# A gated attention and mixture-of-experts block: two expert steps between the last attention stages, the gating and maximum products in another order, and the residual added last

## What is computed

```python
x = x + tanh(g_xattn) * attention(layernorm(x), ctx, ctx)   # 32 query heads of 16, 8 key/value heads
z = layernorm(x)
logits = tanh(z @ Wg1.T) @ Wg2.T                            # 8 experts
scores = softmax over the two largest logits, 0 elsewhere
h = silu(z @ Wup[e].T + bup[e]);  y_e = h @ Wdown[e].T + bdown[e]
x = x + tanh(g_ffn) * sum over e of scores[e] * y_e
```

## Time and profile before

| what | before |
|---|---|
| timed runs, median | 796.16 us |
| the profiled execution | 791.42 us |
| its span, first to last instruction | 789.6 us |
| mean granted TensorE clock | 0.946 |
| TensorE busy | 675.6 us |
| VectorE busy | 551.0 us |
| ScalarE busy | 380.1 us |
| GpSimd busy | 293.7 us |

### The profile page before, as it was taken

One profiled execution on the slowest core, in us unless ns is written; L12 is line 12 of the kernel. 1 busy time (PEld: TensorE's weight loads), 2 busy tenths in 40 slices (PEclk: granted clock), 3 DMA queues, 4 the chain that ended last, 5 costly groups with the idle time before them and its releaser, 6 DMA issues.

```text
span 789.6 us, 17887 instructions
## 1 busy us (share of the span) xinstructions
PE 675.6 (86%) x5232; PEld 463.6 (59%) x5232; DVE 551.0 (70%) x1541; ACT 380.1 (48%) x706; POOL 293.7 (37%) x406
## 2 busy tenths in 40 slices
PE   3789999999999999998889699999999998979600
PEld 2445545455455554554443488889998997768500
DVE  3567878778787787878873466777766766766635
ACT  2366766666676666766653133333333334433300
POOL 4123445454454545545432400000000026665564
PEclk9999999999999999999996689999999999898955
DMA  4622434344443443434221754444456468999898
GB/s 152 211 84 88 140 129 137 125 141 137 129 138 123 141 137 127 137 126 139 71 104 54 271 189 155 151 144 156 145 167 201 148 228 270 312 326 305 280 350 277
DMA packets 67847, 135.15 MB, mean 171 GB/s; under 512 B 8640, under 2 KB 12736, under 8 KB 67520
## 3 DMA queue, kind: packets, MB, share of 16 engines
q1 hardware_dynamic: 46432, 81.28, 30.8%
q0 software_dynamic: 10240, 33.56, 12.4%
q10 hardware_dynamic: 11104, 19.42, 8.0%
HBM read 76.04 MB, written 58.20 MB: 170 GB/s over the span
## 4 chain that ended last, share of the span: by engine, by line
PE 69%; DVE 14%; DMA 8%; POOL 3%; issue 3%; ACT 1%; DVEq 0%; SPq 0%; POOLq 0%
PE s_ps L987 12%; DVE nmax L770 10%; PE bank_a L966 8%; PE st_ps L1010 7%; DMA r_in<-x_scratch 5%; PE st_ps L1120 4%; PE st_ps L1121 4%; PE st_ps L1122 4%; PE bank_c L1027 4%; PE s_ps L1104 4%; DMA out<-r_in 3%; PE bank_b L975 3%; PE st_ps L1018 2%; POOL y_late L514 2%; PE bank_b L1133 2%
## 5 line engine op out<-in xcount | busy, mean ns | idle before, releaser
L770 DVE TENSOR_REDUCE nmax<-s_ps 128x8 f32<-128x1024 f32 x128 | 156.2, 1220 | 83.7 <-PE s_ps L987 83.3
L545 ACT ACTIVATE probs<-st_ps 128x1024 f32<-128x1024 f32 x128 | 131.2, 1025 | 109.7 <-PE st_ps L1018 106.1
L987 PE MATMUL s_ps<-k_t,q_t 32*128 32x256 f32 x1024 | 151.6, 414 | 35.4 <-DVE nmax L770 32.7
L1010 PE MATMUL st_ps<-q_t,k_t 32*128 32x512 f32 x512 | 147.9, 652 | 0.8 <-ACT probs L545 0.7
L987 PEld LDWEIGHTS s_ps<-k_t,q_t 32*128 32x128 f32 x1024 | 92.1, 191 | 86.0 <-DVE nmax L770 47.3
L493 POOL DMA_INDIRECT y<-expert_out,rows_all x42 | 41.3, 983 | 193.1 <-DMA expert_out<-y_sb 183.4
L1120 PE MATMUL st_ps<-w_hi,zh 128*128 x312 | 96.0, 308 | 0.6 <-DVE zl L891 0.6
L1121 PE MATMUL st_ps<-w_lo,zh 128*128 x312 | 88.9, 285 | 0.0
L1122 PE MATMUL st_ps<-w_hi,zl 128*128 x312 | 88.6, 284 | 0.0
L629 ACT ACTIVATE t_sb<-u_sb 128x256 f32<-128x256 f32 x78 | 32.6, 418 | 104.5 <-DVE u_sb L899 104.5
L470 POOL DMA_INDIRECT slots<-z,slot_i x64 | 64.2, 1004 | 16.4 <-issue 16.1
(11 more groups left out here) (149 smaller groups left out, 1420.3 us busy)
## 6 DMA issues: line engine op xcount, KB each, us to landing
expert_out<-y_sb SPq DMA_DIRECT2D x78, 256.0 KB, 2.8
z_s<-slots ACTq DMA_DIRECT2D x74, 256.0 KB, 2.7
x_in<-in_x SPq DMA_DIRECT2D x32, 256.0 KB, 2.7
wst<-in_w SPq DMA_DIRECT2D x32, 256.0 KB, 2.6
x_res<-in_x SPq DMA_DIRECT2D x32, 256.0 KB, 2.9
x_scratch<-x_res SPq DMA_DIRECT2D x32, 256.0 KB, 2.0
r_in<-x_scratch SPq DMA_DIRECT2D x21, 256.0 KB, 4.6
out<-r_in SPq DMA_DIRECT2D x21, 256.0 KB, 4.5
```

The costliest lines, as they stand in the source:

```text
L545: a.activation(out, st_ps[:, :].rearrange("t (k n) -> t k n", k=2), ACT.Exp, scale=HD ** -0.5).then_inc(exp_done[half], 1)
L770: v.tensor_reduce(out, s_ps[:, :].rearrange("s (r g c t) -> s r g c t", r=2, g=2, c=2), X_AXIS, ALU.max, negate=True).then_inc(max_done, 1)
L987: last = t_.matmul(s_ps[:, HALF * rr + 2 * P * gg:HALF * rr + 2 * P * (gg + 1)], q_t[r2][row:row + ROWS32, P * g_:P * (g_ + 1)], k_t[r2][r ...
L1010: t_.matmul(st_ps[:, HALF * rr:HALF * (rr + 1)], k_t[r][row:row + ROWS32, P * i:P * (i + 1)], q_t[r][row:row + ROWS32, :], start=True, sto ...
```

## The change

It has three parts.

1. In the attention steps the gating layer stands elsewhere: the first gating product behind `scores(1)` and the ranking, the second behind `scores(2)`; ScalarE's tanh behind the copy of the attention output; VectorE's copy of the logits behind z and MAX8 behind the reciprocal. In each score block the maximum product comes first on its array rows, then the transposed scores, and the last pair of `s_ps` is issued last.
2. Expert steps 1 and 2 are run between attention steps 36 and 37 and between 37 and 38, before the barrier; the second part starts with step 3. For this `zh`, `zl`, `u_sb`, `t_sb`, `hh`, `hl` and `y_sb` get memory over attention buffers that are free by then, with waits for those.
3. In mixing y2 is gathered first and scaled as before; VectorE computes y1 = y1 * coefficient + y2 one step later, without the residual; GpSimd adds the residual. Stores and residual loads stand one step later, and the mixing runs from step 58 to 80.

```diff
 def mixed_at(s):
-    return [... MIX0 + m * (TILES + 3 - MIX0) // (NA - 1) == s]
+    return [... MIX0 + m * (TILES + 2 - MIX0) // (NA - 1) == s]
...
 # SyncE
-                for m in mixed_at(s - 2 if isinstance(s, int) else s):
+                for m in mixed_at(s - 3):
                     store_mixed(m)
-                for m in mixed_at(s - 3 if isinstance(s, int) else s):
+                for m in mixed_at(s - 4):
...
 # GpSimd
-                for j, (y, done, read) in enumerate(((y1, y1_loaded, mix1), (y2, y2_loaded, mix2))):
+                for j, (y, done, read) in enumerate(((y2, y2_loaded, mix1), (y1, y1_loaded, mix2))):
...
+                    pool.wait_ge(r_loaded[n % RRING], 16 * (n // RRING + 1))
                     pool.wait_ge(mix1, n + 1)
-                    pool.wait_ge(scaled, n + 1)
-                    g.tensor_tensor(r_in[n % RRING][:, :], r_in[n % RRING][:, :], y2[n % YRING][:, :],
+                    g.tensor_tensor(r_in[n % RRING][:, :], r_in[n % RRING][:, :], y1[n % YRING][:, :],
...
 # VectorE
-                for m in mixed_at(s):
...
-                    dve.wait_ge(r_loaded[m % RRING], 16 * (m // RRING + 1))
+                for m in mixed_at(s - 1):
+                    dve.wait_ge(scaled, m + 1)
                     dve.wait_ge(y1_loaded[m % YRING], 16 * (m // YRING + 1))
-                    v.scalar_tensor_tensor(r_in[m % RRING][:, :], y1[m % YRING][:, :], coef[0][:, m:m + 1],
-                                           r_in[m % RRING][:, :], ALU.mult, ALU.add).then_inc(mix1, 1)
+                    v.scalar_tensor_tensor(y1[m % YRING][:, :], y1[m % YRING][:, :], coef[0][:, m:m + 1],
+                                           y2[m % YRING][:, :], ALU.mult, ALU.add).then_inc(mix1, 1)
...
 # TensorE (the other engines alike)
-            pipeline(pe, step, STEPS, LOOP0, NA + O_SLOT, RING)
-            pe.drain().then_inc(phase1_over, 1)
-            pe.wait_ge(phase1_over, 4)
...
+            pipeline(pe, step, STEPS - 2, LOOP0, NA + O_SLOT, RING)
+            pe.wait_ge(tab_done[0], 2)
+            pe.wait_ge(max_done, 4 * B)
+            tile_step(1, 1, False)
+            step(STEPS - 2, (STEPS - 2) % RING)
+            pe.wait_ge(exp_done[0], 2 * B)
+            pe.wait_ge(exp_done[1], 2 * B)
+            pe.wait_ge(w_lo_done, B)
+            tile_step(2, 2, False)
+            step(STEPS - 1, (STEPS - 1) % RING)
+            pe.drain().then_inc(phase1_over, 1)
+            pe.wait_ge(phase1_over, 4)
+            tile_pipeline(pe, tile_step, 3)
```

More of the change, by code:

```diff
@@ L74, in pipeline, with tile_pipeline @@
         step(s, s % unroll)
-def tile_pipeline(eng, step):
-    for s in range(TILES + 4):
+def tile_pipeline(eng, step, first=0):
+    for s in range(first, TILES + 4):
         step(s, s % 16, s == 0)
@@ L93, in mixed_at @@
 def mixed_at(s):
-    return [m for m in range(NA) if isinstance(s, int) and MIX0 + m * (TILES + 3 - MIX0) // (NA - 1) == s]
+    return [m for m in range(NA) if isinstance(s, int) and MIX0 + m * (TILES + 2 - MIX0) // (NA - 1) == s]
 def block_kernel(nc, x_d, ctx_d, gx_d, gf_d, wg1_d, wg2_d, w_d, bup_d, bdn_d, out_d):
@@ L164, in block_kernel @@
         nmax = [sb(f"nmax{i}", [P, H], F32, p1) for i in range(2)]
-        nm_parts = sb("nm_parts", [P, D], BF16, p1)
-        nm_t = [sb(f"nm_t{i}", [P, D], BF16, p1) for i in range(2)]
         tooth = sb("tooth", [P, PAIRS], F32, p1)
@@ L202, in block_kernel @@
         bdn = sb("bdn", [P, E * D], F32, p23)
+        zh = [sb(f"zh{i}", [P, D], F32R, p23) for i in range(2)]
+        zl = [sb(f"zl{i}", [P, D], F32R, p23) for i in range(2)]
+        u_sb = [sb(f"u_sb{i}", [P, HE], F32, p23) for i in range(2)]
+        t_sb = [sb(f"t_sb{i}", [P, HE], F32, p23) for i in range(2)]
+        hh = [sb(f"hh{i}", [P, HE], F32R, p23) for i in range(2)]
+        hl = [sb(f"hl{i}", [P, HE], F32R, p23) for i in range(2)]
+        y_sb = [sb(f"y_sb{i}", [P, D], F32, p23) for i in range(2)]
         r_in = [sb(f"r_in{i}", [P, D], F32, p23) for i in range(RRING)]
@@ L387, in _ @@
             for s in (TILES + 4, TILES + 5):
-                for m in mixed_at(s - 2):
+                for m in mixed_at(s - 3):
                     store_mixed(m)
@@ L595, in step @@
                     a.activation(w_hi[:, bass.ds(s * WCHUNK, WCHUNK)], wst[:, :], ACT.Copy).then_inc(w_hi_done, 1)
-            pipeline(act, step, STEPS, LOOP0, NA + O_SLOT, RING)
-            act.wait_ge(gap_done, B)
-            act.drain().then_inc(phase1_over, 1)
-            act.wait_ge(phase1_over, 4)
-            act.wait_ge(tab_done[0], 2)
-            for b in range(NA - RING, NA):
-                act.wait_ge(scattered[b % RING], ring4(b, b % RING, 32))
-            a.activation(egap[:, :], gap_all[:, :], ACT.Exp).then_inc(exp2_done, 1)
             def tile_step(s, u, fresh):
@@ L635, in tile_step @@
                                  scale=coef[1][:, m:m + 1]).then_inc(scaled, 1)
-            tile_pipeline(act, tile_step)
+            pipeline(act, step, STEPS - 2, LOOP0, NA + O_SLOT, RING)
+            act.wait_ge(pv_done, 2 * B)
+            act.wait_ge(on_done, 2 * B)
+            act.wait_ge(st_done[1], 2 * B)
+            act.wait_ge(nmt_done, B)
+            act.wait_ge(tab_done[0], 2)
+            for b in range(NA - RING, NA):
+                act.wait_ge(scattered[b % RING], ring4(b, b % RING, 32))
+            tile_step(1, 1, False)
+            step(STEPS - 2, (STEPS - 2) % RING)
+            tile_step(2, 2, False)
+            step(STEPS - 1, (STEPS - 1) % RING)
+            act.wait_ge(gap_done, B)
+            act.drain().then_inc(phase1_over, 1)
+            act.wait_ge(phase1_over, 4)
+            a.activation(egap[:, :], gap_all[:, :], ACT.Exp).then_inc(exp2_done, 1)
+            tile_pipeline(act, tile_step, 3)
         @block.vector
@@ L1046, in step @@
                 if valid(b6):
+                    pe.wait_ge(zt_copied, b6 + 1)
+                    for c in range(DC):
+                        last = t_.matmul(bank_c[0:E, 0:S], wg1[:, c * E:(c + 1) * E], z_t[:, P * c:P * c + P],
+                                         start=(c == 0), stop=(c == DC - 1))
+                    last.then_inc(lg1_done, 1)
+                scores(2)
+                if valid(b6):
                     pe.wait_ge(th_done, b6 + 1)
                     t_.matmul(bank_c[:, 0:E], th_sb[:, :], wg2[:, :], start=True, stop=True).then_inc(lg2_done, 1)
-                scores(2)
                 if valid(b4):
```

85 lines of the change are left out of this document (39 added, 46 removed).

## The result

The changed kernel takes 818.7 us (median of 4 runs, 818.1 to 819.3), the kernel before 796.15: a ratio of 1.028 (95% interval 1.023 to 1.033). Some executions of every kernel have a lower mean clock and take longer, and the ratios leave them out. The changed kernel is slower by 2.8%; I forecast 785, and the time lies outside my range. Its profiled execution took 818.1 us, span 816.3, where the one before had 789.6.

What follows compares the result with a forecast made beforehand. TensorE was taken to bound attention, with attention stages, seam and mixing to price: -6.8 + 0 + 1.5 - 6 = -11.3 us, from 791.4 to 780 profiled, 785 us as timed median; range 774 to 806.

Steps and rivals of the forecast that it cites:

- Maximum products moved, 0: Attention score blocks: reordering products inside one group of array rows costs nothing; good-side bound -6 us.
- the equal 0.97 us: Score blocks: transposed scores to maximum product take 0.97 us with or without score pairs, read as groups not slowing one another.
- score pairs in order: Rival, attention: each block's last score pair ends 0.23 us later, giving +9.7 us in all, 806 us; chance 0.15.
- My bound of 0.23 a block: Score blocks, bad side: the last score pair waits its turn and ends 0.23 us later.
- clock: Rival, mixing: spread waits keep TensorE at 1.2 GHz longer, 14 more us at half clock cost 7: 792; chance 0.1.
- Gating layer moved, -0.27 a stage: Attention: -0.55 + 0.25 + 0.03 us a stage over 25 stages, -6.8 us; bounds -13.8 and 0.
- the context transpose's 0.03: Attention stage: the context transpose waits 0.03 us more for VectorE's logits copy, ready at 3.24 against TensorE's 3.21.
- The cover of the first gating product: Attention, between score blocks 1 and 2: ranking and first gating product end at 313.15, just before block 2 at 313.25.
- Seam, +1.5: Attention to experts: running the first two expert steps early costs more than it hides, +1.5 us; bounds -2.8 and +3.1.
- Mixing, -6: Mixing: adding the residual last on GpSimd saves half of a possible 0 to 12 us.
- mixing gives nothing: Rival, mixing: ScalarE waits for the y2 gather instead of VectorE's residual wait, DMA share stays 0.89: 791; chance 0.2.
- the 0.93 that I looked for: Sign of being right, mixing: DMA share of 0.93 or more from 650 us to the end of the tiles.

Runs made afterwards that it cites:

- e1: Kernel before with only the maximum products moved (first in their group, last score pair issued last): 796.4 us, ratio 1.001.
- e10: Kernel before with gating layer, mixing and early expert steps changed, and two small GpSimd products between its scatters; maximum products as before: 785.5 us, ratio 0.986.
- e8: Changed kernel with two 128x1 products added on GpSimd between its two scatters: 799.7 us, ratio 1.003.
- e14: Kernel before with gating layer and mixing changed, two GpSimd products between scatters, and VectorE's logits copy right behind the third maximum: 775.1 us, ratio 0.972.
- e6: Changed kernel with the maximum products alone put back as before: 789.7 us, ratio 0.992.
- e13: Changed kernel with four 128x1 products ahead of GpSimd's first scatter: 814.4 us, ratio 1.019.
- e17: Kernel before, unchanged, profiled again: 794.8 us.
- e7: Kernel before with gating layer and mixing changed, the other two edits left out: 787.0 us, ratio 0.990.
- e2: Kernel before with the gating layer alone moved: 793.6 us, ratio 0.998.
- e3: Kernel before with expert steps 1 and 2 alone put between the last attention stages: 798.4 us, ratio 1.002.
- e9: Kernel before with gating layer and mixing changed, and two 128x1 GpSimd products between its scatters: 784.3 us, ratio 0.985.
- e4: Kernel before with the mixing alone changed: 791.5 us, ratio 0.994.
- e5: Kernel before with gating layer and maximum products both moved, early expert steps and mixing as before: 816.3 us, ratio 1.022.
- e18: Changed kernel with two GpSimd products between the scatters (as e8), profiled again: 797.7 us.

## Why the prediction was wrong

Distances between the starts of the score blocks, medians of six batches (12, 15, 16, 19, 20, 23; all six are late in the changed kernel), show where each step of mine went:

| us from block to block | 1 to 2 | 2 to 3 | 3 to 4 | 4 to 1 | stage |
|---|---|---|---|---|---|
| before | 3.63 | 2.50 | 3.66 | 2.50 | 12.29 |
| e1 (products) | 3.53 | 2.65 | 3.61 | 2.65 | 12.44 |
| e10 (gating layer, scatters apart) | 3.00 | 2.50 | 4.16 | 2.50 | 12.16 |
| e8 (both, scatters apart) | 3.00 | 2.65 | 4.31 | 2.65 | 12.61 |
| after | 2.99 | 2.65 | 4.31 | 3.34 | 13.31 |
| e14 (copy early) | 3.00 | 2.50 | 3.75 | 2.50 | 11.75 |

- **Maximum products moved, 0: this step failed, and it decides.** I took the equal 0.97 us between two products of one group, with and without score pairs beside them, for independence of the groups. It only says that they stream side by side. The last score pair waits its turn behind the transposed scores: the maximum starts 1.37 us behind its block, not 1.22, and the exponential, which now waits for those transposed scores, comes just ahead of it at 1.31. The rule that I cited against me ("TensorE: Matmul & The Clock Gate", Part 3, The mechanism, of the Trainium skill) has matmuls end in program order, and these starts agree with it. Putting the products alone back in the changed kernel (e6) takes 29 us off by the ratios. In e8 it costs 0.45 us a stage against e10, in three blocks, as my rival "score pairs in order" had it, at 0.15 each and not 0.23. Alone (e1) it costs a third, since the transposed scores end earlier and two other distances shrink. My bound of 0.23 a block was wide enough for this; I gave it 0.15 of the chances. By the ratios e10, the change without this step and with the scatters apart, has -11.5 us, e8 +2.4 and the changed kernel +22: so the order costs 14 us by itself and 20 more by what follows.
- **What neither forecast nor rival had** is the last column: 2.65 to 3.34, the late signal. The later signal (1.37) and GpSimd's second scatter (with the gating layer moved it starts 1.33 us behind the block, before 1.55) met within 0.1 us. With the scatters apart the profiled execution has 9.2 us less by the last query transpose, which the 15 delays of 0.55 to 0.73 us account for, and 12.0 less in the drain, which runs at half clock from 433.8 us on in the one and nearly all at full in the other. The first part is shown to be the late signals' doing. The second isn't: e13 has the slow drain without them, so its cause stays open. The rival "clock" looked for a loss in the mixing and there was none (0.99 from 680 to 780 us; the kernel before had 0.93 from 650 to 750 in the earlier trace rows and 0.98 in e17); it came in the drain.
- **Gating layer moved, -0.27 a stage.** The first distance gained 0.63 (I had 0.55), the third lost 0.50 where I had 0.28: of the thin margins, the context transpose's 0.03 was 0.26 in e7 and 0.49 in the row of 280.64. Net it is -0.13. (The stages of the kernel before that I took as 12.24 each are 12.25 to 12.45, 12.32 in the mean; that changes little.) In e2 the late exponential and the slightly late maximum hide it (its stage is 12.33 in these batches): 1.7 us in all, which isn't told from nought. Moving the copy gives more than the rest: -0.54 a stage in e14. The cover of the first gating product held, as the row of 275.79 shows.
- **Seam, +1.5.** 1.2 between the last z transpose and the first expert result. The gating product of batch 31 starts at 473.17, 4.1 us behind the last z transpose, where it was 1.15 (440.7 to 441.85): 2.9 late where I had 3.6. Alone it is +3.1 with an interval that holds nought (e3), and beside the other edits +1.2 (e10 against e9), which isn't told from nought either.
- **Mixing, -6.** -3.9 in e4 (interval 0.3 to 0.8% of the time). VectorE's 19.7 us of waiting are gone. GpSimd waits 13.2 us for the residual, and ScalarE, which waited 0.6 us for its gather, now waits 15.9 ahead of its scaling, as the rival "mixing gives nothing" had it, but for less than VectorE had. The DMA share from 680 to 780 us is 0.90, under the 0.93 that I looked for. ScalarE's scaling in the changed kernel:

```profile
L628 ACT ACTIVATE y<-y,coef 128x512 f32<-128x512 f32 x21 | 15.1, 718 | 15.9 <-DMA y<-expert_out,rows_all 11.8 <-issue 4.1
```

Three of the four steps together came near the whole sum that I forecast (e10: -11.5 us, mine -11.3), in part by luck, since their single sizes differ from mine and e10 has the scatters apart as well. The rest of the loss is one step put at nothing and an interaction, and a sum of single steps has no place for an interaction.

## What to carry to other kernels

Put the matmul whose signal the next engine waits for ahead of others in program order, even if they use other rows of the array. Two edits that are each worth nothing can cost 20 us together (e1, e2 and e5); part of it here is that they move two engines against each other by a few tenths. So look at what else is issued within 0.1 us of a signal on the critical path, and measure edits in pairs as well as alone. Where two indirect DMAs follow each other at once beside such a path, try a gap between them. And take more than one profile of a kernel before pricing its stages: two of the kernel before differ by 0.25 us a stage.

## What was not expected of the hardware

- Semaphore signals of TensorE often come late when they fall due 1.0 to 1.5 us behind the start of a GpSimd scatter: by 0.1 to 0.3 us if due up to 1.31 behind it, and by 0.6 to 0.7 if due later and a second scatter starts at 1.34 (15 of 20 such blocks in the changed kernel). With the second at 1.69 none of 16 was late by that (e8, e18), and with only a first scatter near (e13) none of 24. TensorE's own next instructions aren't delayed (1.19 to 2.02 us behind the block's start in all 24 stages).
- More work on GpSimd shortened the program by some 20 us (818.7 to 799.7, ratios 1.028 and 1.003).
- In every profile of the kernels with both moves and no gap between the scatters 58 to 72 us around the drain (380 to 500 us) were at half clock, and 17 to 34 in the others. e13 had no late signals and still had it.
